# A graph network and slice attention on one core: the one-hots of the next turn's first block written in two halves

## The reference, cut to what is computed

```python
# x (6250, 256) float32; src, dst (106250,): edges, sorted by dst, with a loop edge for each node
n = layernorm(x)
agg = segment_sum(n[src], dst)                      # rows of n summed by destination
h = relu(agg @ W_rel + b_rel + n @ W_root)          # 512 wide
i, f, g, o = split(h @ W_ih.T + b_ih + b_hh, 4)
x = x + (sigmoid(o) * tanh(sigmoid(i) * tanh(g))) @ W_fc + b_fc
m = layernorm(x)
w = softmax(((m @ W_x + b_x) @ W_slice + b_slice) / temp)    # 8 heads of 64 slices, for each node
tokens = sums over all nodes of (m @ W_fx + b_fx) times w, over the sums of w
x = x + (w @ attention(tokens)) @ W_out + b_out     # w is used again for every node
```

## Time and profile before

| | |
|---|---|
| time, median of 3 runs (lowest, highest) | 1250.91 us (1247.07, 1253.03) |
| profiled execution: its own time | 1246.6 us |
| its span | 1244.8 us |
| mean granted clock of TensorE | 0.989 |
| busy, share of the span | PE 89%, DVE 67%, POOL 64%, ACT 50% |

### The profile page before, as it was taken

The page is one execution under the profiler, slowest core; times in us unless marked ns, Lnnn a source line. Parts: engine busy times, 40 slices in busy tenths (PEclk is TensorE's granted clock), DMA queues, the critical chain, the costliest instruction groups (busy, mean ns, idle before and its releaser), DMA issues. The chain is left out here.

```text
span 1244.8 us, 30252 instructions
## 1 busy us (share of the span) xinstructions
PE 1113.5 (89%) x9821; PEld 970.4 (78%) x9821; DVE 833.0 (67%) x2580; ACT 627.7 (50%) x1257; POOL 793.0 (64%) x836
## 2 busy tenths in 40 slices
PE   1056889999999999999999999999999999999998
PEld 0045778788888887888888877888888888897798
DVE  7885466677566856776667666766676667646665
ACT  6862435545454545544554455445645554545332
POOL 5367777777777777777777777777777777400000
PEclk9997899999999999999999999999999999999999
DMA  9574444544554445444544454444444554223498
GB/s 329 205 248 120 123 117 147 150 133 122 150 150 140 128 139 148 139 128 136 150 142 138 126 150 139 141 126 148 140 140 127 148 147 137 90 60 99 129 347 291
DMA packets 92942, 188.74 MB, mean 152 GB/s; under 512 B 20890, under 2 KB 55567, under 8 KB 92797
## 3 DMA queue, kind: packets, MB, share of 16 engines
q0 software_dynamic: 39168, 107.01, 30.4%
q1 hardware_dynamic: 42770, 59.89, 14.8%
q10 hardware_dynamic: 10859, 20.05, 4.5%
HBM read 154.87 MB, written 32.00 MB: 150 GB/s over the span
## 5 line engine op out<-in xcount | busy, mean ns | idle before, releaser
L676 POOL DMA_INDIRECT ring<-table,sidx x798 | 765.3, 959 | 266.0 <-issue 260.3
L414 PE MATMUL ps<-h_h,wih_h 128*128 128x250 f32 x1200 | 338.2, 282 | 0.0
L415 PE MATMUL ps<-h_l,wih_h 128*128 128x250 f32 x1200 | 336.0, 280 | 0.0
L416 PE MATMUL ps<-h_h,wih_l 128*128 128x250 f32 x1200 | 336.0, 280 | 0.0
L414 PEld LDWEIGHTS ps<-h_h,wih_h 128*128 128x128 f32 x1200 | 229.6, 191 | 2.0 <-issue 0.8
L415 PEld LDWEIGHTS ps<-h_l,wih_h 128*128 128x128 f32 x1200 | 229.6, 191 | 1.1
L416 PEld LDWEIGHTS ps<-h_h,wih_l 128*128 128x128 f32 x1200 | 229.5, 191 | 0.0
L820 ACT ACTIVATE gate<-ps,bgate 128x250 f32<-128x250 f32 x300 | 124.4, 468 | 138.3 <-PE ps L416 138.3
L1048 PE MATMUL ps<-ring,oneh 128*32 128x512 f16 x2280 | 147.3, 386 | 46.3 <-DMA ring<-table,sidx 35.5
L1475 DVE TENSOR_SCALAR oneh<-iota,didx 128x64 f16<-128x64 f16 (+2 forms) x1199 | 183.5, 259 | 0.9 <-issue 0.9
L1048 PEld LDWEIGHTS ps<-ring,oneh 128*32 128x32 f16 x2280 | 61.3, 97 | 114.4 <-DMA ring<-table,sidx 48.0
(11 more groups left out here) (212 smaller groups left out, 2499.2 us busy)
## 6 DMA issues: line engine op xcount, KB each, us to landing
sp_ring<-table SPq DMA_DIRECT2D x1920, 1.0 KB
ring<-table,sidx POOLq DMA_INDIRECT x798
swt_d<-swt ACTq DMA_DIRECT2D x25, 500.0 KB
gate<-swt_d SPq DMA_DIRECT2D x19, 500.0 KB, 5.7
x_room<-in_x SPq DMA_DIRECT2D x12, 512.0 KB, 10.5
xn<-table SPq DMA_DIRECT2D x25, 224.0 KB
xin<-in_x SPq DMA_DIRECT2D x25, 224.0 KB
res<-xin SPq DMA_DIRECT2D x25, 224.0 KB
```

What stands on the lines that cost most here:

```text
L414: eng.matmul(dst, wh, xh, start=first, stop=False)
L415: eng.matmul(dst, wh, xl, start=False, stop=False)
L416: return eng.matmul(dst, wl, xh, start=False, stop=last)
L676: pool.indirect_dma_start(ring[:, j, :], None, table, bass.IndirectOffsetOnAxis(ap=idx, axis=0)).then_inc(done, 16)
```

## The change

`hots` takes a part. Part 0 waits for `sum_done` and writes the first half of the block's chunks; part 1 writes the rest and signals `hot_done`. In the turns that have both `ahead` and `ffn` (turns 2 to 23, 22 of them) part 0 stands where all of the one-hots stood, and part 1 stands behind `low_sw`. Turns 0 and 1 are as they were, and turn 24 and those behind it have no such one-hots.

```diff
-            def hots(b):
+            def hots(b, part=None):
 
                 e, (plan, _) = b % 2, hot_plan(b)
-                after(dve, sum_done[e], b // 2)
-                for j, (w0, w1, at) in plan.items():
+                half = len(plan) // 2
+                chunks = list(plan.items())[(part or 0) * half:half if part == 0 else len(plan)]
+                if part != 1:
+                    after(dve, sum_done[e], b // 2)
+                for j, (w0, w1, at) in chunks:
                     n = WIN * (w1 - w0)
                     last = dve.tensor_scalar(oneh[:, e, at:at + n], iota[:, WIN * w0:WIN * w1], didx[:, j:j + 1],
                                              -float(WN * b), ALU.subtract, ALU.is_equal)
-                last.then_inc(hot_done[e], 1)
+                if part != 0:
+                    last.then_inc(hot_done[e], 1)
...
                 if ahead:
-                    hots(2 * t + 2)
+                    hots(2 * t + 2, 0 if ffn else None)
                 if ffn:
                     softmax_end(t - 2)
...
                 if ffn:
                     low_sw(t - 2)
+                    if ahead:
+                        hots(2 * t + 2, 1)
```

## The result

| | before | changed |
|---|---|---|
| median of 6 runs (lowest, highest) | 1251.6 us (1247.07, 1253.08) | 1256.3 us (1255.11, 1258.03) |
| profiled execution: time, span | 1246.6, 1244.8 us | 1255.11, 1253.3 us |
| busy time of the 798 gathers | 765.3 us | 773.5 us |
| span less that busy time | 479.5 us | 479.8 us |

The ratio is 1.0042, 95% interval 1.0023 to 1.0061: the change costs some 5 us, which lies inside the 0.5% that was called the same, but the median of 1256.3 us is 0.1 us above the range that was given. TensorE's granted clock is 0.989 in both profiled executions, so the difference is not the clock's. PE's waits moved as worked out. The gathers did not stay: 8.2 of the 8.5 us between the two spans are in their durations.

The account below looks back on a forecast made before the run. It took POOL's row of gathers as the bound. Instructions 0, PE's replaced waits 0 and gathers 0 summed to 0, so it forecast the unchanged median, 1250.9 us, range 1244.8 to 1256.2 us.

Parts of the forecast that it names:

- The bound: POOL's gathers set the turn, one begins every 1.271 us; PE has 0.86 us of slack in a turn.
- the moved wait: PE's 0.67 us wait at L1125 moves to L1063 and L414; 14.7 us of waits replaced, net 0.
- Rivals A and B: A: PE's wait was the bound, 1236.2 us, 5%. B: second half delays `hl_lo`, 1274.7 us, 5%.
- The gathers: Change in POOL's gather durations from DVE instructions running at their start: taken as 0, bounds -6.1 to +5.3 us.
- rival C: Gathers' stretch shifts through the port pair DVE and POOL share: 1244.8 to 1256.2 us; 12% beyond 3 us.
- the moved pair: DVE's `cell_o` and `cell_c` at 510.88 and 511.21 us, moved by 1.94 us against the gathers' 1.25 us beat.
- `cell_o(2)` to `low_hl` stay: On DVE, these stand behind everything swapped; with no idle time there, they end at the same times.
- The bound of 0.24 us: Upper bound for the gathers: one more stretch of 1.19 - 0.95 = 0.24 us in each of 22 turns, +5.3 us.
- The waits for gathered rows stay near 18 us: Sign of being right: PE's waits for gathered rows between 226 and 1064 us, 18.1 us before, hardly change.
- the last wait for rows: PE's wait at 1063.35 us, block 48, turn 24; a move of over 6 us would make the forecast wrong.
- The sign named for C: Gathers' busy time between 226 and 1064 us leaving 629 to 641 us would show shifted stretch.
- The range: Forecast time range 1244.8 to 1256.2 us, from the bounds on the gathers' stretch, also holding the runs' scatter.

Follow-up runs that it names:

- the second profiles: The kernel before and the changed kernel, both unchanged, each profiled once more: spans 1247.8 and 1253.0 us.
- e8: Changed kernel with only `cell_o(1)` and `cell_c(2)` reading one input from PSUM, values not the LSTM's; ratio to the kernel before 1.0028.
- e15: Changed kernel with part 1 of the one-hots behind `cell_c(3)`, ahead of `cell_o(3)`; ratio to the kernel before 1.0099.

## Why the prediction was wrong, and where it was right

- **The bound** was read rightly: POOL's row of gathers sets the turns, and the table shows it to within 2.8 us of 20.6. But "nothing any other engine does holds POOL back in a turn" is wrong: DVE does, by 7.3 us between 160 and 1062 us even in the kernel before.
- **The instructions that the change adds: 0**, and **the moved wait: 0.** Both right. The 14.0 us at L1125 (21 turns) went, and 10.8 + 5.8 = 16.6 us at L1063 and L414 came. `cell_o(2)` kept its distance from `cell_c(1)`: 516.03 - 506.17 = 9.86 us in the changed profile for 9.77 us. ACT's wait fell to 8.6 / 20 = 0.43 us.
- **Rivals A and B** did not happen, by the marks that were named for them: no earlier end, and DVE idle ahead of the sum for 0.6 us once and ahead of `low_sw` for 0.8 us in two turns together, under the 0.9 us named.
- **The gathers: 0, with bounds of -6.1 and +5.3 us.** This is the step that failed; rival C had named the mechanism, but at the wrong instructions. It measured +8.2 us in the first two profiles, +4.9 us in the second two, and +4.7 us between the medians. "I take 0, since the pair is as likely to be over a gather's start after as before" took the moved pair as the only thing that changes, and "`cell_o(2)` to `low_hl` stay" was true of their times and not of what stands ahead of `cell_c(3)`: ACT's gates 10 and 11 came 1.8 us sooner, behind the `low_sw` that the prediction had itself moved. From then on every gather that met `cell_o(2)` was held through `cell_c(3)` too, and `low_hl`'s first instruction met 14 gathers for 6. These two places have 7.4 us of stretch for 2.5 us before (6.2 for 2.1 us in the second profiles), the moved pair 1.9 for 1.0 us, and e8 shows that most of the loss stays without the pair. The prediction also took both instructions of the pair to hold the gather at 510.92 us; it ended at 512.11 us, 0.82 us behind `cell_o(1)`, so `cell_c(2)` had no part in it.
- **The bound of 0.24 us** for a stretch was the longest that the old profile's row showed, 1.19 us. The new order made a form that it did not show, a gather held through two instructions, up to 1.59 us. The +5.3 us was near the medians' 4.7 us by luck: it was added up as one stretch of 0.24 us in every turn, and the growth came from 8 gathers of 0.5 to 0.64 us and smaller ones elsewhere.
- **The signs.** "The waits for gathered rows stay near 18 us" failed (24.9 us), and so did the last wait for rows: the one at 1063.35 us is gone, and the one a turn ahead of it moved from 1021.97 to 1030.31 us, by 8.3 us where 6 us were allowed. The sign named for C could not tell: the gathers' busy time between 226 and 1064 us is 638.4 us, inside its 629 to 641 us, because longer gathers leave room for fewer (660 for 665). Per gather it shows: 967 ns for 955 ns.
- **The range** was the median of three runs plus the bounds, with no room for the scatter of that median. With the six runs' 1251.6 us it would have ended at 1256.9 us and held the result; the miss of 0.1 us says little, the term of the gathers was wrong all the same.

## What to carry to other kernels

When GpSimd's indirect DMAs are the bound, VectorE's instructions with two SBUF inputs cost time even when VectorE is idle a third of the time, and in two places here (`cell_o(2)` with `cell_c(3)`, and `cell_o(3)` with `add_bfc` in e15) far more when two or three of them followed each other with nothing to wait for. Subtract the gathers' busy time from the span before explaining a difference: if what is left is constant, look for what holds the gathers, and read it per gather, not in a window. A reorder that brings an input sooner can cost, since it takes away a late wait that had let another engine in.

## What was not expected of the hardware

- A gather of 0.95 us that starts while such an instruction runs ends 0.81 to 0.83 us behind that instruction, in each of 773 cases, and so the next gathers begin at a fixed distance from it. That is why the first instruction of `low_hl` met a gather 14 times in the changed profile and 6 times in the old one, with the same instructions around it.
- Whether a pair holds a gather through both was all or none at a given pair of a kernel (0 of 25 and 35 of 35 at `cell_o(2)`), and not only by whether a wait stands between them.
- Two executions of one program differ by 3.0 us of span, of which 2.8 us is in the gathers.
